# Query and key bias placed in PSUM by VectorE before the products, in a fused adaLN, linear attention and mixture-of-experts block

## The reference, cut to what matters

```
h = _layernorm(x) * (1 + ca) + sa
Q = _feature_map(h @ Wq.T + bq)      # _feature_map(t) = elu(t) + 1
K = _feature_map(h @ Wk.T + bk)
V = h @ Wv.T + bv
KV = einsum('bshd,bshe->bhde', K, V);  K_sum = K.sum(axis=1)
x = x + ga * (attention of Q, KV, K_sum, through Wo and bo)
x = x + gb * ffn(_layernorm(x) * (1 + cb) + sb)
```

## Time and profile before

| what | us |
|---|---|
| median of three runs | 365.79 |
| the profiled execution, whole | 366.65 |
| its span | 364.6 |
| TensorE products busy | 349.9 |
| VectorE busy | 286.7 |
| GpSimd busy | 260.5 |
| ScalarE busy | 234.0 |

### The profile page before, as it was taken

One profiled execution on the slowest core, in us unless ns is written; L12 is line 12 of the kernel. 1 busy time (PEld: TensorE's weight loads), 2 busy tenths in 40 slices (PEclk: granted clock), 3 DMA queues, 4 the chain that ended last, 5 costly groups with the idle time before them and its releaser, 6 DMA issues.

```text
span 364.6 us, 8796 instructions
## 1 busy us (share of the span) xinstructions
PE 349.9 (96%) x2780; PEld 327.3 (90%) x2780; DVE 286.7 (79%) x820; ACT 234.0 (64%) x516; POOL 260.5 (71%) x358
## 2 busy tenths in 40 slices
PE   7999999998999996899999999999999999999995
PEld 7877888887888996899998999999999999999895
DVE  4769767567776989989999898898898988886754
ACT  4376787888978764648557485584674855855541
POOL 4346899877977667787897878889889877655210
PEclk9999999999999999999999999999999999999999
DMA  7941640000000032142240322422314314324211
GB/s 267 331 155 34 202 144 0 2 1 2 0 2 3 1 119 89 40 135 89 61 144 21 127 90 60 135 79 78 104 54 131 87 58 145 89 59 146 93 54 58
DMA packets 23713, 31.79 MB, mean 87 GB/s; under 512 B 2288, under 2 KB 14204, under 8 KB 23680
## 3 DMA queue, kind: packets, MB, share of 16 engines
q1 hardware_dynamic: 23240, 31.34, 27.6%
q10 hardware_dynamic: 440, 0.04, 0.1%
HBM read 27.04 MB, written 4.34 MB: 86 GB/s over the span
## 4 chain that ended last, share of the span: by engine, by line
PE 75%; DVE 16%; issue 4%; DMA 2%; ACT 2%; DVEq 0%; ACTq 0%
PE bank L795 21%; PE bank L796 19%; PE bank L797 19%; PE bank L803 4%; PE bank L850 3%; DVE hid_g L1348 2%; PE bank L827 2%; DMA g_bc<-in_b 2%; DVE bank L1365 2%; PE bank L978 2%; DVE early L1265 1%; PE bank L903 1%; DVE gT_f L1404 1%; PE bank L1020 1%; DVE den L1296 1%
## 5 line engine op out<-in xcount | busy, mean ns | idle before, releaser
L738 ACT ACTIVATE bank<-bank,cols_sb 128x256 f32<-128x256 f32 x128 | 51.3, 438 | 43.1 <-PE bank L797 42.8
L795 PE MATMUL bank<-tr_hi,w_hi 128*128 128x256 f32 x256 | 73.4, 287 | 0.0
L796 PE MATMUL bank<-tr_lo,w_hi 128*128 128x256 f32 x256 | 72.3, 282 | 0.0
L797 PE MATMUL bank<-tr_hi,w_lo 128*128 128x256 f32 x256 | 72.1, 282 | 0.0
L795 PE MATMUL bank<-w_hi,hid_pair 128*128 128x256 f32 x252 | 70.6, 280 | 0.0
L797 PE MATMUL bank<-w_hi,hid_pair 128*128 128x256 f32 x252 | 70.4, 279 | 0.0
L796 PE MATMUL bank<-w_lo,hid_pair 128*128 128x256 f32 x252 | 70.4, 279 | 0.0
L501 POOL TENSOR_TENSOR hid_pair<-hid_g,hid_pair 128x512 fp32r<-128x512 f32 x42 | 54.3, 1294 | 7.0 <-POOL gT_r L526 3.3
L795 PEld LDWEIGHTS bank<-tr_hi,w_hi 128*128 128x128 f32 x256 | 48.8, 191 | 0.3 <-DVE hid_g L1348 0.2
L797 PEld LDWEIGHTS bank<-tr_hi,w_lo 128*128 128x128 f32 x256 | 48.9, 191 | 0.0
L796 PEld LDWEIGHTS bank<-tr_lo,w_hi 128*128 128x128 f32 x256 | 48.8, 191 | 0.0
(11 more groups left out here) (161 smaller groups left out, 934.0 us busy)
## 6 DMA issues: line engine op xcount, KB each, us to landing
g_bc<-g_dram SPq DMA_DIRECT2D x64, 256.0 KB, 3.5
x_sb<-in_x SPq DMA_DIRECT2D x16, 256.0 KB, 3.7
out<-x_sb SPq DMA_DIRECT2D x15, 256.0 KB, 2.3
early<-in_wmod SPq DMA_DIRECT2D x3, 512.0 KB, 7.4
q_sb<-in_w SPq DMA_DIRECT2D x2, 512.0 KB, 6.4
q_sb<-in_w SPq DMA_DIRECT2D x1, 1024.0 KB, 10.3
mod_row<-mod_dram SPq DMA_DIRECT2D x1, 1024.0 KB, 6.6
q_sb<-in_wqkvT SPq DMA_DIRECT2D x2, 384.0 KB, 5.7
```

Source lines behind the costliest of these rows:

```text
L738: last = ac.activation(half, half, ACT.Gelu, bias=b1_sb[:, e:e + 1])
L795: te.matmul(out_ap, l_hi, r_hi, start=start, stop=False, skip_group_check=shared)
L796: te.matmul(out_ap, l_hi, r_lo, start=False, stop=False, skip_group_check=shared)
L797: return te.matmul(out_ap, l_lo, r_hi, start=False, stop=stop, skip_group_check=shared)
```

## The change

The bias row is no longer split and multiplied. One load copies it to all 128 partitions (`bqk_bc`, 128 x 512 float32, 256 KB in place of two rows of 2 KB). VectorE copies that tile into the bank ahead of a unit's products (`set_bias`), and the products accumulate on it: none of them has the start flag, and the last one of the six ends the group. Two products at the very start (`all_set`) write banks 2 and 3 once, so that later products add to what lies there; the filling products move to bank 6. `set_bias(u+1, 0)` stands between the two feature maps of unit u and `set_bias(u+1, 1)` behind the second. On TensorE the wait for the feature map becomes a wait for `set_bias`. On ScalarE `exp_qk(u, 0)` moves ahead of `modulate(u+1)` and its cast.

```diff
-            act.dma_start(bqk_raw[0:1, :], rows[:, 0:2 * E]).then_inc(d_bias, 16)
-            act.dma_start(bqk_raw[32:33, :], rows[:, 0:2 * E]).then_inc(d_bias, 16)
+            act.dma_start(bqk_bc[:, :], rows[0, 0:2 * E].partition_broadcast(P)).then_inc(d_bias, 16)
...
                 negative_part(u, 0)
+                exp_qk(u, 0)
                 if u.plus(1):
                     modulate(u.plus(1), u.plus(1).batch())
                 if u.plus(1) and cast_late(u.plus(1)):
                     cast_activations(u.plus(1))
-                exp_qk(u, 0)
...
-            act.wait_ge(zero_rows, 1)
-            act.wait_ge(d_bias, 32)
-            ac.activation(bqk_t[32:33, :], bqk_raw[32:33, :], ACT.Copy).then_inc(bqk_step, 1)
-            ac.activation(bqk_r[0:1, :], bqk_raw[0:1, :], ACT.Copy).then_inc(bqk_step, 1)
...
-                wait(pe, a_fm, u.count(2, t - 1))
+                wait(pe, a_bias, u.count(2, t + 1))
                 for c in range(NC):
-                    mm3(bank[2 + t][:, :], tr_hi[:, h, c, tok], tr_lo[:, h, c, tok],
-                        wqkv_hi[:, c, 0:2 * E], wqkv_lo[:, c, 0:2 * E], c == 0, False)
...
-                te.matmul(bank[2 + t][:, :], ones_r[:, :], bqk_r[:, :], start=False, stop=True).then_inc(a_qk, 1)
+                    last = mm3(qk_bank(u, t)[:, :], tr_hi[:, h, c, tok], tr_lo[:, h, c, tok],
+                               wqkv_hi[:, c, 0:2 * E], wqkv_lo[:, c, 0:2 * E], False, c == NC - 1, True)
+                last.then_inc(a_qk, 1)
...
+            for t in range(2):
+                last = te.matmul(bank[2 + t][:, :], b2_r[:, 0:P], gT_r[:, :, :].rearrange("p t n -> p (t n)"),
+                                 start=True, stop=True)
+            last.then_inc(all_set, 1)
...
-            for rows in (bqk_r[:, :], b2_r[:, :], gT_r[:, :, :], g_nat[:, :, :]):
+            for rows in (b2_r[:, :], gT_r[:, :, :], g_nat[:, :, :]):
...
+            def set_bias(u, t):
+
+                wait(dve, a_fm, u.count(2, t - 1))
+                ve.tensor_copy(qk_bank(u, t)[:, :], bqk_bc[:, :]).then_inc(a_bias, 1)
...
-            dve.wait_ge(bqk_step, 2)
-            TT(bqk_r[32:33, :], bqk_raw[32:33, :], bqk_t[32:33, :].bitcast(F32), ALU.subtract).then_inc(bqk_ready, 1)
+            dve.wait_ge(d_bias, 16)
+            dve.wait_ge(all_set, 1)
+            for t in range(2):
+                set_bias(u0, t)
...
+                if u.plus(1):
+                    set_bias(u.plus(1), 0)
                 feature_map(u, 1)
+                if u.plus(1):
+                    set_bias(u.plus(1), 1)
```

More of the change, by code:

```diff
@@ L128, in adaln_block @@
         setup_f = g_bc[:, :, :, :].rearrange("p s j n -> p (s j n)")
-        bqk_raw, bo_raw = setup_f[0:33, 0:2 * E], setup_f[0:B, 2 * E:3 * E]
+        bo_raw = setup_f[0:B, 2 * E:3 * E]
         b2_raw = setup_f[0:NE, 3 * E:4 * E]
         mod_of = setup_f[0:B, 4 * E:8 * E].rearrange("b (k e) -> b k e", k=4)
-        bqk_t = setup_r[0:33, 2 * n_qkv:2 * n_qkv + 2 * E]
         b2_t = setup_r[0:NE, 2 * n_qkv + 2 * E:2 * n_qkv + 3 * E]
         gate_sign, gate_abs, gate_size = (q_sb[0:B, 8 + 2 * k:10 + 2 * k, :] for k in range(3))
-        bqk_r = sb("bqk_r", [P, 2 * E], F32R)
+        bqk_bc = sb("bqk_bc", [P, 2 * E])
         cols_sb = sb("cols_sb", [P, NC * 2 * NE + NC + NE])
@@ L212, in adaln_block @@
         a_bo = sem("a_bo")
-        bqk_step = sem("bqk_step"); bqk_ready = sem("bqk_ready")
+        a_bias = sem("a_bias"); all_set = sem("all_set")
         a_st = sem("a_st"); a_eps = sem("a_eps"); a_stats = sem("a_stats"); a_pow = sem("a_pow"); a_rstd = sem("a_rstd")
@@ L269, in weights_late, with qk_bank @@
             return any(u.nth(j) for j in range(UPB + 1, UPB + 4))
+        def qk_bank(u, t):
+            return bank[2 + t]
         def norm_bank(u):
@@ L818, in qk @@
                 tok = slice(t * P, (t + 1) * P)
-                wait(pe, a_fm, u.count(2, t - 1))
+                wait(pe, a_bias, u.count(2, t + 1))
                 for c in range(NC):
-                    mm3(bank[2 + t][:, :], tr_hi[:, h, c, tok], tr_lo[:, h, c, tok],
-                        wqkv_hi[:, c, 0:2 * E], wqkv_lo[:, c, 0:2 * E], c == 0, False)
-                if u.nth(0) and t == 0:
-                    pe.wait_ge(ones_ready, 1)
-                    pe.wait_ge(bqk_ready, 1)
-                te.matmul(bank[2 + t][:, :], ones_r[:, :], bqk_r[:, :], start=False, stop=True).then_inc(a_qk, 1)
+                    last = mm3(qk_bank(u, t)[:, :], tr_hi[:, h, c, tok], tr_lo[:, h, c, tok],
+                               wqkv_hi[:, c, 0:2 * E], wqkv_lo[:, c, 0:2 * E], False, c == NC - 1, True)
+                last.then_inc(a_qk, 1)
             def v(u):
@@ L882, in _ @@
             pe.wait_ge(zero_rows, 1)
+            for t in range(2):
+                last = te.matmul(bank[2 + t][:, :], b2_r[:, 0:P], gT_r[:, :, :].rearrange("p t n -> p (t n)"),
+                                 start=True, stop=True)
+            last.then_inc(all_set, 1)
             for _ in range(WARM[0]):
-                te.matmul(bank[3][:, 0:E], b2_r[:, 0:P], b2_r[:, :], start=True, stop=True)
+                te.matmul(bank[6][:, 0:E], b2_r[:, 0:P], b2_r[:, :], start=True, stop=True)
             pe.wait_ge(d_wmod[0], 16)
@@ L902, in _ @@
             for _ in range(WARM[1]):
-                last = te.matmul(bank[3][:, 0:E], b2_r[:, 0:P], b2_r[:, :], start=True, stop=True)
+                last = te.matmul(bank[6][:, 0:E], b2_r[:, 0:P], b2_r[:, :], start=True, stop=True)
             last.then_inc(warm_done, 1)
@@ L923, in sum_k @@
                 pe.wait_ge(a_kst, UPB * (b + 1) + 1)
+                pe.wait_ge(ones_ready, 1)
                 pe.wait_ge(cent_n2_ready, 1)
```

## The result

The changed kernel takes 367.09 us (median of 20 runs, 366.14 to 368.89) where the kernel before, in 20 runs beside it, takes 365.78 (365.11 to 366.67). The ratio is 1.0034, 95% interval 1.0024 to 1.0044. The 7.4 us of products are gone and the kernel is not faster. The profiled execution took 366.36, with a span of 364.5; that of before took 366.65 and 364.6. These two are not typical of their kernels: 366.65 lies at the upper end of the runs of before (highest 366.67) and 366.36 in the lower half of the changed kernel's, so the two spans differ by -0.1 us where the medians differ by +1.3.

What follows compares the result with a forecast made beforehand. TensorE was taken to set the pace, only 0.3 to 0.4 us a unit ahead of a loop through all four engines. Stage A -0.1 and start +0.7 gave +0.6 us: median 365.79 becomes 366.3, range 363.8 to 368.8.

Steps and rivals of the forecast that it cites:

- the three chances: Whole kernel: faster (under 364.7 us) 0.26, slower (over 366.9 us) 0.33, otherwise no change; 0.3% is 1.1 us.
- The copy: VectorE, SBUF to PSUM, 128x512: takes 0.69 us, adds 0.60 to VectorE's queue.
- The removal: TensorE, 16 units: two bias products fewer in each, 7.4 us of its time.
- Stage A: All 16 units: nearly all of the 7.4 us removed turns into waiting, sum -0.1 us.
- The loop of units 3 to 7: Each unit takes 5.88 (even) to 6.07 us (odd), mean 5.97 against 5.91; five units: +0.3.
- the moved Exp: ScalarE, units 3 to 7: it costs 0.62 us ahead of `modulate`; the missing product gives back 0.23.
- VectorE as the bound: Rival, units 2 to 7: +0.4 us a unit for six units, start +1.3, time 369.2; chance 0.25.
- cheap copies: Rival: the copy takes 0.42 us; sum about -1.4, time 364.4; chance 0.15.
- `modulate` in odd units: ScalarE, units 3 to 7: computing the batch's registers adds up to 0.2 us before `modulate` in odd units.
- Two branches: Ahead of the next unit's first product: `modulate`, cast, `split_lo` with 0.34 us slack; feature map with 0.84.
- the start: Before unit 0: 256 KB more, queued ahead of the small loads, costs +0.7 us, bounds 0 and 1.5.
- the two `all_set` products: TensorE at the start: cost 2 x 0.45 us; one cleared tile less gives part back, the rest is hidden.

Runs made afterwards that it cites:

- order_alone: The kernel before with only ScalarE's order changed, `exp_qk(u, 0)` ahead of `modulate(u+1)`: 367.31 us, ratio 1.0045.
- mixed_order: The changed kernel with the bias load last in ScalarE's queue and the Exp behind `modulate` again in units 0 to 7: 365.63 us, ratio 1.0008.
- bias_load_last: The changed kernel with the 256 KB bias load issued behind the three small loads: 365.99 us, ratio 1.0009.
- half_short_add_bo: half_copies with GpSimd's addition of the bias row to x cut to 8 of 256 columns in units 2 to 9: 364.10 us, ratio 0.9933.
- tiny_copies: The changed kernel with the bias copies cut to 8 of 512 columns: 365.26 us, ratio 0.9981.
- half_copies: The kernel before with only the bias of `qk(u, 1)` as a copy, old ScalarE order, load last in its queue: 364.61 us, ratio 0.9945.

## Why the prediction was right, and where it was not

The forecast was 366.3 against 367.09, inside both ranges (363.8 to 368.8, and 365.0 to 367.6); the sum itself, 365.79 + 0.6, is 366.4. At 1.0034 the kernel is slower by just over the bound of 0.3% that the text set; the likeliest of the three chances, no change at 0.41, missed that by little.

**Right.** The copy (0.694). The removal (TensorE's busy time fell by 8.1 us, 7.4 or so forecast). Stage A, where 7.4 us turn into waiting: -0.15 against -0.1, with every term within 0.2. The loop of units 3 to 7 at 5.94, inside 5.88 to 6.07, with waits put down in turn to the copy and to `split_lo`. That the moved Exp costs is shown by order_alone (+1.6 us); with the copies in place, taking it back gives 0.12 in each of units 3 to 7 (mixed_order against bias_load_last) and nothing that can be measured in the whole time; VectorE as the bound (units at 6.2 and more) did not come true, nor did cheap copies.

**Off: `modulate` in odd units.** In unit 7 it moved by 0.23, at the low end of 0.24 to 0.44. The 0.2 charged to odd units for the batch's registers doesn't show there: `modulate` starts 0.53 behind the Exp (63.24, 63.77). That goes with units 3 to 7 at +0.14 and not +0.3.

**Off: what holds the loop.** Two branches were followed; there is a third, through the statistics and GpSimd's rstd. The prediction named it for units 9 to 11 only. Two cuts of GpSimd's work that left the loop's mean as it was, and the waits that took their place, point to it, and in one unit of half_short_add_bo it is seen to end last; it was not taken away by itself.

**Off: the start.** The step that failed is that the small loads behind the new one would be late. The wait is on the `early` weights in another queue; the load alone moves the kernel by 1.9 over the runs, beyond the bound of 1.5 (in the profiled executions it moves unit 0 by 1.4 to 2.5 us, 17.39 against starts of 16.02 to 14.84 without it). And the two `all_set` products were taken as a cost, partly hidden; with the load there, the earlier and longer beginning likely gives back about half of it (1.0022 against 1.0051). Both errors point in opposite ways, so that the sum hides them: that 366.3 came within 0.8 us of 367.09 is in part luck. Over all runs the start is dearer than in the profiled execution: half of them lie 1.2 us higher.

**Not forecast: the end.** The changed kernel gives back 0.44 us behind stage A, although no code there differs. The other profiles say that this is not chance: in the six kernels with both bias copies (in tiny_copies 8 columns wide) that stretch takes 244.24 to 244.45 us, in the eight with one or none 243.87 to 244.18. I have no experiment on it; the cause stays open.

## What to carry to other kernels

When the busiest engine is only a few per cent ahead of a loop through the others, removing its work is worth what the loop has in slack: leave that work out altogether first (here 4.2 us of 7.4, by the ratio), since a replacement that only adds work elsewhere can hardly beat that. Then move only the part whose result is due late, and leave alone the order of what the loop waits for: one copy in place of two, with nothing reordered and the load last in its queue, gained 0.55% where the full exchange lost 0.34%. A full in-order queue in a profile is no proof of a bound: shorten it, and see whether a wait takes the gap.

## What the runs showed of the hardware

While a broadcast of one 2 KB row to 128 partitions ran, 256 KB in all, the DMA engines moved half (361 to 180 GB/s, at busy shares of 1.10 and 0.98), and the first of the weight loads in another queue landed at 7.6 us in place of 5.7 (1.31 + 6.31 against 1.30 + 4.4).

TensorE's 16 small products took 0.22 us each in the kernel before (5.7 to 9.3 us, granted clock 1.00, which is 2.4 GHz) and 0.12 in the changed kernel; there the granted clock was then 0.50 (1.2 GHz) from 10 to 16 us. Which of the two a profile shows isn't settled by the code: half_copies and half_short_add_bo start alike and took 2.00 and 3.41 us for them, and the first then has a clock of 0.50 from 10 to 16 us, the second 1.00.
